# Reordering the projection, convolution and carry-over work of a Mamba-2 plus mixture-of-experts kernel

## The reference

```python
# layer 1, per sequence of 512 tokens
zxbcdt = x @ Win.T                      # z: 256, xBC: 512, dt: 4 columns
xBC = silu(causal_conv4(xBC) + conv_b)  # per channel; x_ssm: 256, B: 128, C: 128
dtp = softplus(dt + dt_bias);  dA = exp(dtp * -exp(A_log))
h_t = dA_t * h_{t-1} + (dt_t * x_t) B_t # 4 heads of 64
y_t = C_t h_t + D x_t
y = rmsnorm(y) * norm_w * silu(z);  x = layernorm(x + y @ Wout.T)
# layer 2: 8 experts, the 2 best by sigmoid gate, FFN 128 -> 512 -> 128 with gelu
x = layernorm(x + sum_e gate_e * (gelu(x W1_e + b1_e) W2_e + b2_e))
```

## Time and profile before

| | |
|---|---|
| median of 3 runs | 702.55 us (701.42 to 702.74) |
| the profiled execution | 699.86 us, its span 698.0 us |
| granted TensorE clock, mean | 0.977 |
| PE busy | 633.0 us (91%), 4811 matmuls |
| PE weight loads | 507.4 us (73%) |
| DVE busy | 542.1 us (78%) |
| ACT busy | 479.5 us (69%) |
| POOL busy | 466.9 us (67%) |

### The profile page before, as it was taken

One profiled execution on the slowest core, in us unless ns is written; L12 is line 12 of the kernel. 1 busy time (PEld: TensorE's weight loads), 2 busy tenths in 40 slices (PEclk: granted clock), 3 DMA queues, 4 the chain that ended last, 5 costly groups with the idle time before them and its releaser, 6 DMA issues.

```text
span 698.0 us, 19510 instructions
## 1 busy us (share of the span) xinstructions
PE 633.0 (91%) x4811; PEld 507.4 (73%) x4811; DVE 542.1 (78%) x1852; ACT 479.5 (69%) x1210; POOL 466.9 (67%) x696
## 2 busy tenths in 40 slices
PE   6789999999999999999998789999999999999900
PEld 4356666666566766666665589999999999999900
DVE  4688898899988998889989577776666666888844
ACT  5567877887787878887786377556665566677724
POOL 5023287788777887788777857777755555777754
PEclk9999999999999999999999999999999999999965
DMA  9280001110111011110110123323422223455352
GB/s 248 56 301 17 13 24 35 39 48 24 38 36 45 29 38 32 44 47 25 35 36 32 43 60 88 92 76 110 98 75 71 74 73 101 137 183 176 122 201 100
DMA packets 56668, 54.50 MB, mean 78 GB/s; under 512 B 9562, under 2 KB 45918, under 8 KB 56304
## 3 DMA queue, kind: packets, MB, share of 16 engines
q1 hardware_dynamic: 45840, 33.67, 17.5%
q0 software_dynamic: 8416, 16.93, 7.1%
q10 hardware_dynamic: 2304, 2.65, 1.1%
HBM read 31.05 MB, written 22.63 MB: 77 GB/s over the span
## 4 chain that ended last, share of the span: by engine, by line
PE 62%; issue 11%; POOL 9%; ACT 6%; DVE 5%; DMA 4%; SPq 1%; DVEq 1%; POOLq 0%; ACTq 0%
PE p L693 12%; PE pl L684 8%; PE pj L512 5%; PE p L684 4%; PE p L756 3%; PE p L727 3%; PE p L781 3%; PE p L750 3%; POOL moe_rows L1772 3%; PE p L802 3%; PE p L767 3%; PE pj L520 2%; PE p L658 2%; PE pj L676 1%; PE pl L533 1%
## 5 line engine op out<-in xcount | busy, mean ns | idle before, releaser
L1772 POOL DMA_INDIRECT moe_rows<-xT x135 | 135.5, 1004 | 78.9 <-DVE xT L1389 49.0
L1696 POOL DMA_INDIRECT sorted_rows<-pair,slot x128 | 128.6, 1005 | 30.6 <-issue 28.4
L1141 DVE SCALAR_TENSOR_TENSOR acc<-pj,conv_w_sb,acc 128x511 f32<-128x511 f32 (+2 forms) x192 | 141.0, 735 | 8.6 <-ACT acc L911 6.8
L693 PE MATMUL p<-w,xT 128*128 x1080 | 143.7, 276 | 2.2 <-ACT xT L1058 1.7
L1058 ACT ACTIVATE xT<-pl,b_sb 128x128 f32<-128x128 f32 x360 | 102.7, 368 | 48.7 <-PE pl L684 46.2
L693 PEld LDWEIGHTS p<-w,xT 128*128 128x128 f32 x1080 | 131.4, 192 | 3.5 <-issue 3.4
L684 PE MATMUL pl<-xT 128*128 128x128 f32 x720 | 95.1, 275 | 1.6 <-DVE xT L1377 1.6
L684 PEld LDWEIGHTS pl<-xT 128*128 128x128 f32 x720 | 87.5, 192 | 1.8 <-issue 1.8
L1385 DVE TENSOR_TENSOR xT<-p,b_sb 128x128 f32<-128x128 f32 x135 | 39.2, 290 | 63.1 <-PE p L693 58.3
L1058 ACT ACTIVATE xT<-p,b_sb 128x128 f32<-128x128 f32 x180 | 51.4, 370 | 23.9 <-PE p L684 23.7
L512 PE MATMUL pj<-xT,w_xbc 128*128 128x512 f32 x128 | 67.2, 607 | 0.0
(11 more groups left out here) (235 smaller groups left out, 1340.2 us busy)
## 6 DMA issues: line engine op xcount, KB each, us to landing
xT<-sorted_rows SPq DMA_DIRECT2D x135, 65.0 KB
xres<-in_x SPq DMA_DIRECT2D x16, 256.0 KB, 3.1
w<-in_w SPq DMA_DIRECT2D x2, 2048.0 KB, 10.0
acc<-moe_rows SPq DMA_DIRECT2D x12, 256.0 KB, 3.8
xT<-moe_rows SPq DMA_DIRECT2D x12, 256.0 KB, 5.4
out<-sz ACTq DMA_DIRECT2D x10, 256.0 KB, 2.4
moe_rows<-xT POOLq DMA_INDIRECT x135, 2.3
sorted_rows<-pair,slot POOLq DMA_INDIRECT x128
```

The source lines that it names most:

```text
L693: mm = pe.matmul(y_bank(j)[:, 0:P], hT[j % 4][:, f, :], w2[:, bass.ds(e, 1), f, :].rearrange("p e d -> p (e d)"), start=(f == 0), stop=(f ...
L1141: ins = dve.scalar_tensor_tensor(out=acc[:, k, j:TOKS], in0=pj[k % 2][:, 0:TOKS - j], scalar=conv_w[:, k, TAPS - 1 - j:TAPS - j], in1=acc[ ...
L1696: pool.indirect_dma_start(out=sorted_rows[:, :], out_offset=bass.IndirectOffsetOnAxis(slot[q.par][:, c, k:k + 1], 0), in_=(rowA, rowB)[k][ ...
L1772: pool.indirect_dma_start(out=moe_rows[:, :], out_offset=bass.IndirectOffsetOnAxis(xs[k][:, P:P + 1].bitcast(I32), 0), in_=ye[j % 8], in_o ...
```

## The change

Five edits, in the entry and in the slots:

1. `ORDER`: projection blocks come in the order B, C, x, x. `inner_products` now waits for two activations, `turn_first_x` for all four.
2. On PE, `inner_products(q)` and (from slot 1 on) `turn_first_x(q)` stand behind the first chunk's output projection, ahead of the three others. Chunk 0's output goes to `p4`, the others to `p5`.
3. On ACT, `keep_products(q)` stands ahead of the skip parts, and both gate parts stand together.
4. `exponents(q, 1)` and its exponentiation move from the next slot's start into chunk 3 of this slot. On PE `project_block(q, 0)` then stands first in chunk 0, ahead of the transpose of B.
5. On DVE, from slot 1 on, `mask_chunk(q, 0)` and `scale_x(q, 0)` (the old `Xdt` lines, now a function) stand ahead of `residual(s)`; on POOL `decay_x(q, 0)` stands ahead of the last scatter.

```diff
+ORDER = (*range(CC, XC), *range(CC))
...
-            return (p5, c * OUTW) if c + 1 < NC else (p4, 0)
+            return (p5, (c - 1) * OUTW) if c > 0 else (p4, 0)
...
# enter_all (PE)
                 steps_of(3)
+                pe.wait_ge(steps_kept, SEQS // GROUP)
+                exponents(q, 1)
                 turn_steps(3)
...
# turn_first_x
-                pe.wait_ge(xc_ready, XC * q.n + CC)
+                pe.wait_ge(xc_ready, XC * (q.n + 1))
...
# inner_products
-                pe.wait_ge(xc_ready, XC * (q.n + 1))
+                pe.wait_ge(xc_ready, XC * q.n + XC - CC)
...
# slot_pe, in the loop over c
-                    if scan and c != 1 and (c + 1 < NC or project):
-                        if not route and c == 0:
-                            pe.wait_ge(steps_kept, SEQS // GROUP)
-                        exponents(s if c + 1 < NC else q, (c + 1) % NC)
+                    if scan and c == 2:
+                        exponents(s, 3)
+                    if project and scan and c == 3:
+                        exponents(q, 0)
+                        exponents(q, 1)
...
                         if c == 0:
+                            if project:
+                                project_block(q, 0)
                             wait(pe, x1_ready, NC * s.n)
-                        if c == 0:
...
-                    if project:
+                    if project and c > 0:
                         project_block(q, c)
...
# slot_pe, the border
                     for c in range(NC):
-                        if c + 1 == NC:
+                        if c == 0:
                             if not route:
                                 pe.wait_ge(decays_ready, 2)
                                 pe.wait_ge(parts_ready, 2)
                                 sums(G0, SEQS, (ones,), 3)
                             elif project:
                                 pe.wait_ge(S_ready, q.n + 1)
-                                turn_first_x(q)
...
+                        if c == 1 and project:
+                            inner_products(q)
+                            if route:
+                                turn_first_x(q)
...
                 if project:
-                    inner_products(q)
                     z_block(q, 1)
...
# slot_act, in the loop over c
-                    if scan and (c + 1 < NC or project):
+                    if scan and 0 < c < NC - 1:
                         exp_exponents(n + 1, c + 1)
+                    if scan and project and c == NC - 1:
+                        exp_exponents(n + 1, 0)
...
                     if scan and c > 0:
                         square(s, c - 1)
+                    if scan and project and c == NC - 1:
+                        exp_exponents(n + 2, 1)
...
                     for k in range(XC):
                         activate(q, k)
+                    keep_products(q)
                     for k in range(CC):
                         skip_part(q, k)
-                    gate_part(q, 0)
-                    keep_products(q)
-                    gate_part(q, 1)
+                    for k in range(CC):
+                        gate_part(q, k)
...
# new function on DVE
+            def scale_x(s, c):
+                dve.wait_ge(tr_psum, NC * s.n + c + 1)
+                wait(dve, Xdd_ready, (NC - 1) * s.n + max(c - 1, 0))
+                o, at = x0_bank(s.n) if c == 0 else (p5, 0)
+                dve.tensor_tensor(heads(Xdt[c % 2][:, :]), heads(o[:, at:at + DI]),
+                                  per_head(cur[s.par][:, 0, :], c), ALU.mult).then_inc(Xdt_ready, 1)
...
# slot_dve
-                if scan:
+                if scan and s.n < 2:
                     dve.wait_ge(cur_ready, s.n + 1)
                     mask_chunk(s, 0)
...
+                if project and s.n > 0:
+                    dve.wait_ge(cur_ready, q.n + 1)
+                    mask_chunk(q, 0)
+                    scale_x(q, 0)
                 if scan:
                     residual(s)
...
# slot_pool
-                if scan:
+                if scan and s.n < 2:
                     pool.wait_ge(cur_ready, s.n + 1)
                     decay_x(s, 0)
...
                 if scatters:
-                    for c in range(2, NC):
-                        scatter(old, c, 1)
+                    scatter(old, 2, 1)
+                if project and s.n > 0:
+                    pool.wait_ge(cur_ready, q.n + 1)
+                    decay_x(q, 0)
+                if scatters:
+                    scatter(old, 3, 1)
```

More of the change, by code:

```diff
@@ L511, in project_block @@
                     wait(pe, conv_done, XC * q.n + k - 1)
-                pe.matmul(pj[k % 2][:, :], w_xbc[:, k * P:(k + 1) * P], xT[:, q.n, :],
+                pe.matmul(pj[k % 2][:, :], w_xbc[:, ORDER[k] * P:(ORDER[k] + 1) * P], xT[:, q.n, :],
                           start=True, stop=True).then_inc(proj_psum, 1)
@@ L910, in tap0 @@
                 wait(act, xc_ready, XC * (q.n - 1) + c + 1)
-                act.activation(acc[:, c, :], pj[c % 2][:, :], ACT.Identity, bias=conv_b[:, c:c + 1],
-                               scale=conv_w[:, c, TAPS - 1:TAPS]).then_inc(tap0_done, 1)
+                act.activation(acc[:, c, :], pj[c % 2][:, :], ACT.Identity, bias=conv_b[:, ORDER[c]:ORDER[c] + 1],
+                               scale=conv_w[:, ORDER[c], TAPS - 1:TAPS]).then_inc(tap0_done, 1)
             def activate(q, k):
@@ L916, in activate @@
                 wait(act, y_psum, NC * (q.n - 1))
-                act.activation(xc[q.par][:, k, :], acc[:, k, :], ACT.Silu).then_inc(xc_ready, 1)
+                act.activation(xc[q.par][:, ORDER[k], :], acc[:, k, :], ACT.Silu).then_inc(xc_ready, 1)
             def skip_part(q, k):
-                act.wait_ge(xc_ready, XC * q.n + k + 1)
+                act.wait_ge(xc_ready, XC * q.n + XC - CC + k + 1)
                 wait(act, yv_ready, NC * (q.n - 1))
@@ L962, in enter_all @@
                 keep_steps(3)
+                exp_exponents(1, 1)
                 enter_dt(1, G0, SEQS)
@@ L1142, in tap @@
                     out=acc[:, k, j:TOKS], in0=pj[k % 2][:, 0:TOKS - j],
-                    scalar=conv_w[:, k, TAPS - 1 - j:TAPS - j], in1=acc[:, k, j:TOKS],
+                    scalar=conv_w[:, ORDER[k], TAPS - 1 - j:TAPS - j], in1=acc[:, k, j:TOKS],
                     op0=ALU.mult, op1=ALU.add)
@@ L1420, in slot_dve @@
                 for c in range(NC):
-                    n = NC * s.n + c
                     if project and c > 0:
                         tap(q, c - 1, 1)
-                    if scan:
[L1426 to L1429, removed]
-                                          per_head(cur[s.par][:, 0, :], c), ALU.mult).then_inc(Xdt_ready, 1)
+                    if scan and (c > 0 or s.n < 2):
+                        scale_x(s, c)
+                    n = NC * s.n + c
                     if route and c == 0:
```

## The result

The changed kernel takes 714.38 us (714.06 to 717.03, 4 runs) against 701.98 us (699.22 to 702.74, 4 runs) for the kernel before in the same session: ratio 1.0188, 95% interval 1.0157 to 1.0219. It is 12.4 us slower where 6.0 were forecast. The direction was right, the forecast size was half of what came, and the time lies above the range.

A forecast was written before the change was run, and what follows sets the result against it. PE was taken to bound the steady slot (0.48 of 22.51 us idle), ACT's sequence its head. +0.33 a slot times 13 = +4.3, plus 1.5 and 0.2, made +6.0: 708.5 us, range 700.5 to 713.5.

The forecast's parts named there:

- point 6: Entry and last slot: entry taken as 0, bounds -0.5 and +1; last border DVE-limited, its mask waiting for `Gm`, +0.2.
- point 5: Slot 0 to 1: sums wait for DVE's `parts`, `Btok` for a later `Xdt`, plus chunk 3's exponents; +1.5 us.
- Point 1: Chunk 3 of a steady slot: six added exponent matmuls cost 0.65, the late weights' 0.27 vanishes; net +0.38 us.
- Point 2: Head of the next slot: ACT's sequence, table load behind the tap, brings L727 at 4.19 against 4.54; -0.35 us.
- the load didn't leave the chain: Rival for the head: table load ahead of `Btok`, while ACT waits for the transpose; 0.40 less per slot, 703.3, chance 0.14.
- PE didn't become the bound: Rival for the head: PE's own work times it, head falls 1.05 instead of 0.35; 699.4, chance 0.10.
- Point 3: Border of a steady slot: PE waits for late Silus and weight loads, plus 0.04 for one more exponentiation; +0.30 us.
- Point 4: Steady slot: everything else moved on ACT, DVE and POOL is hidden, costing nothing while gaps of 0.3 to 1 us last.
- DVE or ACT slips in the border: Rival: `Gm` or Silu of z block 0 0.3 to 0.5 us later, +0.7 to +0.8 a slot; 713, chance 0.12.

The follow-up runs named there:

- exps_only: Kernel before plus only the moved exponents of chunk 1 and their exponentiation, block 0 first in chunk 0: 745.66 us against 741.75, ratio 1.0058.
- border_only: Changed kernel with the exponents' move and block 0's new place undone: 750.26 us against 741.75 for the kernel before, ratio 1.0114.
- inner_at_2: Changed kernel without the exponents' move, inner products and first x behind two output chunks instead of one: 747.95 us against 741.16 for the kernel before, ratio 1.0088.
- gt2_early: Kernel before plus the exponents' move, POOL's gated output of chunk 2 ahead of two scatters: 702.94 us against 701.15, ratio 1.0017.
- sz_first: Changed kernel with the Silu of z block 0 ahead of ACT's skip parts: 712.34 us against 701.15 for the kernel before, ratio 1.0147.
- last_old: Changed kernel with slot 14's border alone in the old order on PE and DVE: 754.47 us against 741.16 for the kernel before, ratio 1.0196.
- entry_old: Changed kernel with the entry's own border in the old order: 755.49 us against 741.16 for the kernel before, ratio 1.0190.
- after_again: Changed kernel run once more, unaltered, on the chip of the later experiments: 715.15 us against 701.15 for the kernel before, ratio 1.0195.
- state_first: Changed kernel with ACT's copy of chunk 0's state ahead of chunk 2's exponentiation: 756.47 us against 741.75 for the kernel before, ratio 1.0197.
- tap_last: Kernel before plus the exponents' move, with ACT's tap of block 0 behind the state copy: 752.06 us against 741.16, ratio 1.0137.
- gt2_and_load: Kernel before plus the exponents' move, POOL's gated output ahead of two scatters, and an early one-element Exp on ACT: 702.05 us against 701.15, ratio 1.0013.

## Why the prediction was half right

The two spans are 8.6 us further apart than the forecast's sum: 3.1 of it lies in the last border (point 6), 3.0 in the steady slots (points 1 to 4), 1.8 in the entry (point 6) and 0.7 in slot 1 (point 5).

**Point 1, exponents in chunk 3: mechanism right, +0.26 for +0.38.** L732 in chunk 3 takes 0.43 us, not 0.70, as said. Another 0.1 came back in the last chunk: from the start of L761 to z block 0 it is 0.58 us, where L756 had 0.68. That this is an earlier `carried` is argued from the rows, not tested.

**Point 2, the head: right.** Table load behind the tap, PE idle 0.97 us before L732, head 0.33 shorter against 0.35, shown by exps_only. Both rivals on this term fell: the load didn't leave the chain, and PE didn't become the bound.

**Point 3, the border: two terms mis-sized.** The waits cost 0.31 for 0.26 (border_only, inner_at_2). "One more exponentiation before the last `ysq` costs 0.04" measured 0.18 (gt2_early): the inserted exponentiation starts at Z + 0.20 and the `ysq` at Z + 0.72, where the step had about Z + 0.1 and Z + 0.57 (214.48 against a Z of 213.91). It took ACT's place in the old order as fixed against Z; but Z itself had moved 0.1 us ahead against ACT's tap (which starts at Z - 1.06 instead of Z - 1.16), as L761 got shorter. By the rows that is most of it.

**Point 4, "hidden": failed in one place.** "Silu of z block 0 ends near Z + 6.8, before block 0 asks for it at Z + 7.15." It ended at Z + 7.14 (205.48) and block 0 asked at Z + 7.36. That is 0.22 us ahead, and still block 0 took 0.16 us more; with the Silu earlier it took 0.86 again (sz_first). The point gave a margin of 0.35 us and named the price if it went; `Gm`, which started at Z + 4.84 and not 4.5, took 0.34 of it. I had priced late weights at 0.27 in the same text and didn't ask for them here. The rest of the point held: mask, `Xdt` and `residual` cost nothing at steady state.

So a steady slot: 0.26 + 0.18 + 0.31 + 0.16 - 0.33 = +0.58, measured +0.56, forecast +0.33. Times 13 that is 3.0 of the 8.6 us between the forecast's sum and the two spans.

**Point 5, slot 0 to 1: +2.2 for +1.5.** The sums wait for `parts` as said. `parts` is done at 61.60, against a Z at 58.07:

```profile
60.95 0.26 DVE L1225 CAST parts<-rest 128x192 bf16<-128x192 f32 x1
61.24 0.36 DVE L1226 TENSOR_TENSOR parts<-rest,parts 128x192 bf16<-128x192 f32 x1
```

That is Z + 3.53, as in the kernel before (59.80 against 56.25). PE comes there 0.91 us too early, where 0.7 was forecast, and the border takes 7.85 instead of 6.74: +1.1. The head takes 5.57 instead of 4.56, +1.0 where +0.5 was forecast: ACT is idle for 1.52 us until the `Xdt` that it needs for `Btok` (68.07, E + 2.15), and the table load (68.36), the tap, the exponentiation and the state copy all stand behind that. In the kernel before, the load was over when `Btok` started (65.43, E + 2.44). The rest grew by 0.07 only, where +0.3 was forecast.

**Point 6, the last border: failed, and it is the largest single term.** "In the last border DVE, not PE, is the limit; its mask now waits for `Gm`: +0.2." Measured 3.3 in the first comparison, 3.7 between last_old and entry_old, 1.7 at the least (after_again against the trace of before); over all traces some 3. The premise was right and its consequence was missed: where DVE is the limit, the order in which PE stands waiting for DVE is what counts. `inner_products` has a second wait (`ms_ready`, a bank to be read first) that the prediction never named. Then the clock fell. In the same point the entry was put at 0, with +1 as its bound; it measured +1.8, and from Z to Z of slot 0 1.8 to 2.2 over five traces. What it left out is again a wait of PE, 2.03 us for the Silu of z block 0, which ACT reaches later, and a longer stretch at 1.2 GHz (entry_old).

The medians' +12.4 and the spans' +14.6 differ because the profiled execution of before lies at the low end of its runs (699.86, median 701.98 in the session of the result).

Among the rivals the one nearest to what happened is "DVE or ACT slips in the border" (713, chance 0.12): its Silu did slip and was paid one for one, but at 2.1 us it made only part of the difference. (Its own sum, +0.7 to +0.8 a slot, gives 713.3 to 714.6, not 713, so that this case stood at the edge of the range and above it.)

## What to carry to other kernels

When work is pulled ahead in a queue, list all the semaphores it waits for, the bank to be read before it is overwritten too, and check each in the first and the last round of the loop, where another engine has extra work: one such border cost about as much as six steady ones. Margins are to be compared with the wait and the late weight load together (of 0.35 us of margin 0.22 were left for a bank that PE asks for, and the block still took 0.16 us longer). Before taking an engine's share out of a stretch that it times, ask what stands behind the moved piece: state_first, tap_last and gt2_and_load shortened the head by 0.84, 0.68 and 0.08 us, and the rest of the slot grew by 0.74, 1.22 and 0.08.

## What the hardware showed that was not expected

- After 2.31 us of PE idle (0.69 us busy in 3) the granted clock fell to 1.2 GHz for 3.4 us, from 0.4 us after the work had begun again; with an idle of 1.53 us inside a stretch of 1.47 us busy in 3 it stayed at 2.4 GHz.
- In the six kernels with edit 4 on the two slower chips DVE's last `yv` of a slot starts 0.3 to 0.4 us after Z, within 0.12 us of the end of POOL's gated output; with edit 4 on the chips with 701 us it starts 0.17 us after Z. In last_old, POOL and DVE in order of time:

```profile
128.68 0.73 POOL L1685 TENSOR_TENSOR gt<-yv,sz 128x256 f32<-128x256 f32 x1
```

```profile
129.38 0.42 DVE L1467 TENSOR_TENSOR yv<-p,xD 128x256 f32<-128x256 f32 x1 [0.45 <-PE p L761]
```

and the same two in the changed kernel, where `yv` starts 0.24 us before POOL's end:

```profile
128.77 0.74 POOL L1678 TENSOR_TENSOR gt<-yv,sz 128x256 f32<-128x256 f32 x1
```

```profile
129.27 0.42 DVE L1464 TENSOR_TENSOR yv<-p,xD 128x256 f32<-128x256 f32 x1 [0.23 <-PE p L761]
```

It costs 0.12 us a slot (border 7.48 and 7.36). That POOL holds DVE back is not shown, and not as a rule: in border_only and inner_at_2, on the same slower chips but without edit 4, `yv` starts 0.07 us after Z and 0.63 us ahead of POOL's end, as in the kernel before. No kernel with POOL's changed order was measured on a slow chip, so the cause stays open.
